# Perceiver block on one core: the next keys' steps one place forward, the next half's exponentials ahead of an eviction, the inverses' broadcast directly behind scores

## The chip, the core and the metric

The kernel runs on one core of a Trainium2 chip. The core has TensorE (PE, the matrix unit, whose weight loads are shown apart as PEld), VectorE (DVE), ScalarE (ACT), GpSimd (POOL) and SyncE (SP, which only starts DMAs here). The metric is the time of one execution on the device in microseconds, the median over runs. Each engine works through its own program in order and waits on semaphores for the others.

## The reference

One layer on `x` (32 images of 64 rows of 256) and a context (32 images of 1601 rows of 256). Most of the time goes into cross attention, which is followed by a small block with cosines and a running product, and by a mixture of experts.

```python
q = _split_heads(query @ Wq.T + bq)          # 16 heads of 16, query = layernorm(x)
k = _split_heads(key @ Wk.T + bk)            # key = value = ctx_1024
v = _split_heads(value @ Wv.T + bv)
score = jnp.einsum('bhqd,bhkd->bhqk', q, k) * SCALE
attn = jax.nn.softmax(score, axis=-1)
out = jnp.einsum('bhqk,bhkd->bhqd', attn, v)
...
x = x + _L0_xattn_ref(_layernorm(x, axis=-1), ctx_1024, ctx_1024, ...)
x = x + _L0_attn_ref(_layernorm(x, axis=-1), ...)
x = x + _L0_ffn_ref(_layernorm(x, axis=-1), ...)
```

The change touches only the cross attention.

## The kernel before

The attention runs over 32 images, and each image in two halves of eight heads: half `h` = 2n + m, 64 halves in all (`NH`). A half has four groups ("quads") i = 0 to 3 of four tiles of scores, 128 x 401 each. The functions named `period(h)`, one for each engine, say what an engine does between two halves; half `h` is finished in it and half `h + 1` is begun.

The way of a group through the engines:

- **Scores.** TensorE multiplies queries and keys (L965, 16 small matmuls on 32 x 32 tiles, into `a_pss`). VectorE takes them out of the four banks (L713, `take_scores`), with the maximum of each row on the way.
- **Maxima.** When all four groups of a half are taken, TensorE turns the row maxima (L974, `turn_max`), VectorE reduces them (L719, `reduce_max`), TensorE spreads the result (L980, `spread_max`), and ScalarE copies it as the bias of the exponentials (L504, `copy_bias`).
- **Exponentials.** ScalarE does four of 128 x 401 for each group (L498). VectorE turns each group (L728, `turn`, into `a_pT`). `a_pT` has 5 places, so the turn of group 1 of a half waits for the weighing of the half before.
- **Weighing.** TensorE multiplies the values by the turned exponentials (L994, `weigh`, 52 matmuls into `a_pso`). The sums of the exponentials are added up by TensorE (L1002, `total`), inverted by VectorE (L736, `invert`), laid out by GpSimd (L348, `spread_sums`), and broadcast by TensorE (L1010, `spread`). ScalarE evicts both (L513, `copy_out`), and GpSimd multiplies them (L357).
- In every fourth period, an odd one, TensorE also projects a finished tile (L1018, `project_out`), and VectorE adds the residual (L742 to L746, `residual`). Such an odd half is called one with a projection here.

In between, TensorE computes the keys and values of the next image in 15 steps, whose order is `STEP_ORDER`: a key step (K) is 6 matmuls of 416 columns, a value step (V) 12 of 256 columns (the last one 6), all on L925 to L927. In the order of the list the steps 0 to 3 are keys of the first half, 6, 8, 9 and 10 keys of the second half, and the others values. Each step fills one of two banks (`a_psk`, `a_psl`) and is copied by ScalarE (L526 keys, L533 and L535 values). A step waits until the step two before it is copied. `steps_in(h)` deals the steps to the four quarters of a period. The scores of group 0 of a half wait until the last key step of that half is copied: step 3 for the first half of an image, step 10 for the second.

```python
last_step = max(z for z, of in enumerate(order_of(n)) if of[0] == "k" and of[1] == m)
pe.wait_ge(kv_copied, STEPS * n + last_step + 1)
...
dve.wait_ge(exp_done, HALF * (at + 1))
if i == 1 and h > 0:
    dve.wait_ge(o_filled, h)
```

The order of all this is written out by hand in the four functions `period`; nothing plans it at run time.

Of the kernel before, what the change touches and what calls it, by code (L numbers as in the profile page):

```python
# [25 lines left out]
NH = NC * B  # L26
# [39 lines left out]
def quads(h):  # L66

    return ((1, 1), (0, 0), (0, 1), (1, 0)) if h % 2 else ((0, 0), (0, 1), (1, 0), (1, 1))
# [7 lines left out]
def steps_in(h):  # L76

    n = h // 2
    if h < 0:
        plan = [[(0, 4), (0, 5), (0, 6)], [(0, 7), (0, 8), (0, 9)], [(0, 10), (0, 11), (0, 12)], [(0, 13), (0, 14), (1, 0)]]  # L80
    elif h % 2 == 0:
        plan = [[(n + 1, 1)], [(n + 1, 2), (n + 1, 3)], [(n + 1, 4), (n + 1, 5)], [(n + 1, 6), (n + 1, 7), (n + 1, 8)]]
    else:
        plan = [[], [(n + 1, 9), (n + 1, 10), (n + 1, 11)], [(n + 1, 12), (n + 1, 13)], [(n + 1, 14), (n + 2, 0)]]
    return [[z for z in quarter if z[0] < B] for quarter in plan]


# [15 lines left out]
def attention_and_circuit(nc, ctxT, x, wq, bq, wk, bk, wv, bv, wp, rows, ident, marks, x1_scr, x1_mv, x1_by, x1_rs, x1_ex, w1, b1, w2, wr, rb, rows_scr,  # L103
                          wgu, wd, tri, counts):
    with ExitStack() as ctx:
# [383 lines left out]
        def _(act):  # L489
            def exponentials(h, i, some=range(HALF)):  # L490

                at = HALF * h + i
                e, r = quads(h)[i]
                act.wait_ge(bias_ready, h + 1)
                for j in some:
                    z = probs[:, at % RING, j, 0:KG]
                    at_bias = HALF * i + j
                    nc.scalar.activation(z, z, ACT.Exp, bias=bias[:, h % 2, at_bias:at_bias + 1], scale=-1.0,  # L498
                                         accum_out=esum[:, h % 2, j, 2 * e + r:2 * e + r + 1]).then_inc(exp_done, 1)

            def copy_bias(h):

                act.wait_ge(max_spread, h + 1)
                nc.scalar.copy(bias[:, h % 2, :], ps_m[:, P:P + HALF * HALF]).then_inc(bias_ready, 1)  # L504

            def copy_out(h):

                act.wait_ge(o_filled, h + 1)
                act.wait_ge(sums_filled, h + 1)
                if h > 1:  # L510

                    act.wait_ge(o_ready, h - 1)
                nc.scalar.copy(o_part[:, h % 2, :], ps_o[:, 0:2 * P]).then_inc(o_copied, 1)  # L513

            def copy_steps(steps):

                for n, s in steps:
                    at = STEPS * n + s
                    act.wait_ge(kv_filled, at + 1)
                    kind, *of = order_of(n)[s]  # L520
                    if kind == "k":
                        m, q = of
                        if n > 0:

                            act.wait_ge(s_filled, HALF * HALF * (NC * (n - 1) + m + 1))
                        nc.scalar.activation(keys[:, m, q * KG:(q + 1) * KG], step_bank(at)[:, 0:KG], ACT.Identity, bias=bk_sb[:, m:m + 1]).then_inc(kv_copied, 1)  # L526
                    else:
                        t = of[0]
                        if n > 1:

                            act.wait_ge(o_filled, NC * (n - 1))
                        if t < KT - 1:
                            nc.scalar.copy(v_of(n)[:, t:t + 2, :], step_bank(at)[:].rearrange("p (t d) -> p t d", t=2)).then_inc(kv_copied, 1)  # L533
                        else:
                            nc.scalar.activation(v_of(n)[:, t, :], step_bank(at)[:, 0:D], ACT.Identity, scale=mark[:, KEPT]).then_inc(kv_copied, 1)  # L535
# [16 lines left out]
            def angles(i):  # L552

                if i == 0 or i == UNITS - 1:
                    act.wait_ge(by_set, 6 if i == 0 else 12)
                act.wait_ge(x1_loaded[group_of[i]], 32 if i == UNITS - 1 else 16)
                if 2 * i + 1 >= KNOWN_IN:

                    act.wait_ge(kv_filled, STEPS * B)
                for t in range(2 * i, 2 * i + 2):  # L560
                    last = nc.scalar.activation(u[:, t, :], x1[:, t, :], ACT.Identity, bias=x1_by[:, 1, t:t + 1], scale=x1_by[:, 0, t:t + 1])
                last.then_inc(centred[0], 1)
# [22 lines left out]
            FORMER, LATTER = range(HALF // 2), range(HALF // 2, HALF)  # L585

            def period(h):
                steps = steps_in(h)
                if h >= 0:
                    exponentials(h, 1)  # L590
                copy_steps(steps[0])
                for i in ANGLES_IN.get((h, 1), ()):
                    angles(i)

                if h >= 0:
                    exponentials(h, 2)
                for i in ANGLES_IN.get((h, 2), ()):
                    angles(i)
                copy_steps(steps[1])

                if h >= 0:
                    exponentials(h, 3)
                for i in ANGLES_IN.get((h, 3), ()):
                    angles(i)
                copy_steps(steps[2])

                if h + 1 < NH:
                    copy_bias(h + 1)
                    exponentials(h + 1, 0, FORMER)
                copy_steps(steps[3][:1])  # L610
                if h > 0:
                    copy_out(h - 1)
                if h + 1 < NH:
                    exponentials(h + 1, 0, LATTER)
                copy_steps(steps[3][1:])

            for h in range(-1, NH):
                period(h)
# [14 lines left out]
            for stage, g in ACT_ORDER:  # L633
# [31 lines left out]
                elif stage == "copy_q":  # L665
                    n = GROUPS[g][1]
# [6 lines left out]
                elif stage == "relu":  # L673
                    i, j, g = g, g % FC, g // FC
                    n = GROUPS[g][1]
# [246 lines left out]
        def _(pe):  # L922
# [6 lines left out]
            def step(n, s):  # L929

                at = STEPS * n + s
                if at > 1:
                    pe.wait_ge(kv_copied, at - 1)
                if s == 0 and n > 0:
                    pe.wait_ge(ctx_split, NC * n)
                bank, slot = step_bank(at), n % 2
                kind, *of = order_of(n)[s]
                if kind == "k":
                    m, q = of
                    for k in range(NC):  # L940
                        mm = three(bank[:, 0:W], [w[:, 0, k, m * P:(m + 1) * P] for w in (w_hi, w_lo)],
                                   [c[:, slot, k].rearrange("p (t g a) -> p g t a", g=QK, a=32)[:, q] for c in (c_hi, c_lo)], k == 0, k == NC - 1)
                else:
                    for t in range(of[0], min(of[0] + TILES_A_STEP, KT)):
                        for k in range(NC):
                            mm = three(bank[:, (t % 2) * D:(t % 2 + 1) * D], [c[:, slot, k, P * t:P * (t + 1)] for c in (c_hi, c_lo)], [w[:, 1, k, :] for w in (w_hi, w_lo)], k == 0, k == NC - 1)
                mm.then_inc(kv_filled, 1)
# [117 lines left out]

            def period(h):
                steps = steps_in(h)

                if h + 1 < NH:
                    scores(h + 1, 2)  # L1070
                if h > 0:
                    weigh(h - 1)
                for z in steps[0]:
                    step(*z)

                if h > 0:
                    total(h - 1)
                if h + 1 < NH:
                    scores(h + 1, 3)
                if h % 4 == 1 and h > 4:  # L1080
                    project_out(h // 4 - 1)
                for z in steps[1]:
                    step(*z)

                if h + 2 < NH:
                    scores(h + 2, 0)
                if h + 1 < NH:
                    if h % 4 == 1 and h > 4:

                        pe.wait_ge(x1_ready, h // 4)  # L1090
                    turn_max(h + 1)
                for z in steps[2][:1]:
                    step(*z)
                if h + 1 < NH:
                    spread_max(h + 1)
                for z in steps[2][1:]:
                    step(*z)

                if h + 2 < NH:
                    scores(h + 2, 1)  # L1100
                for z in steps[3][:1]:
                    step(*z)
                if h > 0:
                    spread(h - 1)
                for z in steps[3][1:]:
                    step(*z)

            for h in range(-1, NH):
                period(h)
# [5 lines left out]
            for stage, g in PE_ORDER:  # L1115
# [8 lines left out]
                elif stage == "turn_q":  # L1124
                    t0, n = GROUPS[g]
# [9 lines left out]
                elif stage == "expand":  # L1135
                    i, j, g = g, g % FC, g // FC
                    t0, n = GROUPS[g]
# [8 lines left out]
                elif stage == "contract":  # L1146
# [5 lines left out]
                    for j in range(2):  # L1152
                        n = 2 * g + j - GROUPS[at][0]
# [678 lines left out]
```

## Time and profile before

| | us |
|---|---|
| median of 3 runs | 1748.42 (1747.88 to 1748.68) |
| profiled execution | 1745.66 |
| its span | 1743.9 |
| TensorE busy in the span | 1651.4 (95%) |
| VectorE busy | 1430.6 (82%) |
| ScalarE busy | 1218.2 (70%) |
| GpSimd busy | 948.6 (54%) |

The attention takes roughly the first 1300 us, some 36 to 37 us for each image. The rows shown below are from one image of the middle, about 699 to 747 us. In a timeline each row has the start, the time to the end of the last instruction of the row, the engine, the line, the operation, and in brackets the idle time ahead of it with what ended it. Matmuls overlap in the pipeline, so the cost of a step on TensorE is read from start to start, not from the length of a row.

### The profile page before, as it was taken

What the parts mean: (1) busy time and instruction counts of PE and PEld (TensorE: products, weight loads), DVE (VectorE), ACT (ScalarE), POOL (GpSimd) and SP (SyncE); (2) the same over time, 40 slices, a digit from 0 to 9 for tenths busy, and PEclk for the clock granted to TensorE, in tenths of its full rate; (3) what the DMA queues carried; (4) which work ended last, traced back from release to release, by engine and by line L of the source; (5) the groups of instructions that cost most, each with busy time, mean ns of one, the idle gap of its engine ahead of it and who ended that gap; (6) DMA issues with size and microseconds to landing.
All of it is one profiled execution on the core that took longest, in us unless ns stands there. A gap on an engine that the chain in (4) does not pass through costs nothing. (4 is left out here: it accounts for less than half of the span.)

```text
span 1743.9 us, 59225 instructions
## 1 busy us (share of the span) xinstructions
PE 1651.4 (95%) x24340; PEld 1352.1 (78%) x24340; DVE 1430.6 (82%) x3316; ACT 1218.2 (70%) x3297; POOL 948.6 (54%) x1427
## 2 busy tenths in 40 slices
PE   7999999999999999999999999996698899999998
PEld 4777777777777777777777777775476899999998
DVE  6698988989889898898888989889775776766657
ACT  3677877778777787777877788777555265656552
POOL 5355556555565555655556555553411448888850
PEclk9999999999999999999999999997797999999999
DMA  5011111211112111121111211111102356666632
GB/s 176 22 64 45 64 48 42 67 45 64 48 42 67 45 64 48 42 67 45 63 49 42 67 45 63 49 45 60 62 25 85 116 180 220 224 223 223 221 122 103
DMA packets 43439, 147.89 MB, mean 85 GB/s; under 512 B 5680, under 2 KB 25008, under 8 KB 39712
## 3 DMA queue, kind: packets, MB, share of 16 engines
q1 hardware_dynamic: 38416, 130.72, 21.9%
q0 software_dynamic: 4752, 13.38, 2.4%
q8 instruction: 192, 3.15, 0.7%
q14 instruction: 79, 0.65, 0.1%
HBM read 129.79 MB, written 14.16 MB: 83 GB/s over the span
## 5 line engine op out<-in xcount | busy, mean ns | idle before, releaser
L498 ACT ACTIVATE a_probs<-a_probs,a_bias 128x401 f32<-128x401 f32 x1024 | 632.0, 622 | 2.1
L728 DVE STREAM_TRANSPOSE a_pT<-a_probs 128x1664 f32<-128x1664 f32 x256 | 488.0, 1906 | 93.5 <-ACT a_probs L498 64.8
L713 DVE TENSOR_SCALAR_CACHE_REDUCE a_probs<-a_pss 128x401 f32<-128x401 f32 x1024 | 527.0, 570 | 25.6 <-PE a_pss L965 8.5
L965 PE MATMUL a_pss<-a_keys,a_qown 32*32 32x401 f32 x8192 | 253.2, 507 | 24.7 <-issue 23.4
L315 POOL TENSOR_TENSOR a_clo<-a_raw,a_chi 128x416 fp32r<-128x416 f32 x240 | 251.5, 1079 | 0.0
L994 PEld LDWEIGHTS a_pso<-a_pT,a_v 128*32 128x32 f32 x6656 | 182.2, 111 | 43.6 <-issue 40.5
L338 POOL TENSOR_SCALAR a_ex<-a_probs,a_marks 128x4 f32<-128x4 f32 x256 | 75.5, 295 | 253.2 <-ACT a_probs L498 252.9
L994 PE MATMUL a_pso<-a_pT,a_v 128*32 128x128 f32 x6656 | 199.7, 277 | 2.5 <-ACT a_op L513 2.1
L1661 PE MATMUL e_psg<-e_xh,e_guh 128*128 128x256 f32 x660 | 189.5, 287 | 5.5 <-DVE e_hl L1407 4.0
L498 ACT ACTIVATION_READ_ACCUMULATOR a_probs<-a_probs,a_bias 128x1 f32 x1024 | 194.4, 190 | 0.0
L1662 PE MATMUL e_psg<-e_xl,e_guh 128*128 128x256 f32 x660 | 186.7, 283 | 0.0
L1663 PE MATMUL e_psg<-e_xh,e_gul 128*128 128x256 f32 x660 | 186.5, 283 | 0.0
L357 POOL TENSOR_TENSOR a_op<-a_op 128x128 f32<-128x128 f32 x64 | 29.5, 461 | 236.8 <-ACT a_op L513 236.8
L1597 ACT ACTIVATE e_sg<-e_psg 128x256 f32<-128x256 f32 x180 | 68.9, 383 | 124.4 <-PE e_psg L1663 120.2
L1400 DVE TENSOR_TENSOR e_psg<-e_psg,e_sg 128x256 f32<-128x256 f32 x180 | 77.6, 432 | 80.7 <-ACT e_sg L1597 78.8
L526 ACT ACTIVATE a_keys<-a_psk,a_bk 128x401 f32<-128x401 f32 x127 | 75.1, 592 | 86.2 <-PE a_psk L927 85.7
L1661 PEld LDWEIGHTS e_psg<-e_xh,e_guh 128*128 128x128 f32 x660 | 125.6, 190 | 6.2 <-issue 6.2
L925 PE MATMUL a_psk<-a_whi,a_chi 128*128 128x256 f32 x420 | 127.3, 303 | 0.0
L1662 PEld LDWEIGHTS e_psg<-e_xl,e_guh 128*128 128x128 f32 x660 | 125.8, 191 | 0.0
L1663 PEld LDWEIGHTS e_psg<-e_xh,e_gul 128*128 128x128 f32 x660 | 125.7, 191 | 0.0
L925 PE MATMUL a_psl<-a_whi,a_chi 128*128 128x256 f32 x412 | 125.3, 304 | 0.0
L526 ACT ACTIVATE a_keys<-a_psl,a_bk 128x401 f32<-128x401 f32 x129 | 76.3, 592 | 64.7 <-PE a_psl L927 64.2
(253 smaller groups left out, 4249.9 us busy)
## 6 DMA issues: line engine op xcount, KB each, us to landing
a_raw<-in_ctxT SPq DMA_DIRECT2D x60, 832.0 KB, 4.4
f_gur<-in_wgu SPq DMA_DIRECT2D x24, 1408.0 KB, 6.5
f_dr<-in_wd SPq DMA_DIRECT2D x24, 768.0 KB, 4.7
e_big<-ys_scr SPq DMA_DIRECT2D x8, 512.0 KB, 7.3
a_probs<-in_ctxT SPq DMA_DIRECT2D x2, 1664.0 KB, 9.3
a_x<-in_x SPq DMA_DIRECT2D x16, 128.0 KB, 4.3
rows_scr<-f_a SPq DMA_DIRECT2D x8, 256.0 KB, 2.3
rows_scr<-f_a SPq DMA_DIRECT2D x4, 512.0 KB, 3.5
```

Source lines behind the costliest of these rows:

```text
L315: last = nc.gpsimd.tensor_tensor(out=c_lo[:, n % 2, k, cols], in0=src[:, cols], in1=c_hi[:, n % 2, k, cols].bitcast(F32), op=ALU.subtract)
L498: nc.scalar.activation(z, z, ACT.Exp, bias=bias[:, h % 2, at_bias:at_bias + 1], scale=-1.0, accum_out=esum[:, h % 2, j, 2 * e + r:2 * e + ...
L526: nc.scalar.activation(keys[:, m, q * KG:(q + 1) * KG], step_bank(at)[:, 0:KG], ACT.Identity, bias=bk_sb[:, m:m + 1]).then_inc(kv_copied, 1)
L713: nc.vector.tensor_scalar(probs[:, at % RING, j, 0:KG], ps_s[:, j, 0:KG], -SCALE, None, ALU.mult, ALU.min, accum_out=nmax[:, h % 2, at_max ...
L728: nc.vector.transpose(pT[:, turned_slot(h, i)].rearrange("p j k -> p (j k)"), probs[:, at % RING].rearrange("p j k -> p (j k)")).then_inc( ...
L925: nc.tensor.matmul(out, a[0], b[0], start=start, stop=False)
L965: mm = nc.tensor.matmul(ps_s[32 * g:32 * g + 32, j, 0:KG], q_own[32 * j:32 * j + 32, n % 2, m, e, 32 * r:32 * r + 32], keys[32 * j:32 * j ...
L994: mm = nc.tensor.matmul(ps_o[32 * j:32 * j + 32, 0:P], v_of(n)[:, t, 32 * p:32 * p + 32], pT[:, h % 2:h % 2 + HALF, j, 32 * t:32 * t + 32] ...
L1400: nc.vector.tensor_tensor(hidden(s, c), up, silu[0:P if c < EC - 1 else REST, c % 2, :], ALU.mult).then_inc(h_done, 1)
L1661: nc.tensor.matmul(out, a[0], b[0], start=start, stop=False)
L1662: nc.tensor.matmul(out, a[0], b[1], start=False, stop=False)
L1663: return nc.tensor.matmul(out, a[1], b[0], start=False, stop=stop)
```

## The change

`steps_in` deals each key and value step one place earlier: in an even period quarter 0 has step 2 instead of 1, quarter 1 has 3 and 4 instead of 2 and 3, quarter 2 has 5 and 6 instead of 4 and 5, quarter 3 has 7, 8 and 9 instead of 6, 7 and 8. In an odd period quarter 1 has 10 and 11 instead of 9, 10 and 11, quarter 2 is unchanged (12 and 13), and quarter 3 has 14 and then steps 0 and 1 of the image after. On TensorE the broadcast of the inverses (`spread`) stands directly behind the scores of quarter 3, ahead of all of that quarter's steps. On ScalarE the copy of the second step of quarter 2 moves behind the first two exponentials of the next half, and the last two exponentials move ahead of the first copy of quarter 3 and ahead of `copy_out`.

```diff
--- before.py
+++ after.py
@@ -77,11 +77,11 @@
 
     n = h // 2
     if h < 0:
-        plan = [[(0, 4), (0, 5), (0, 6)], [(0, 7), (0, 8), (0, 9)], [(0, 10), (0, 11), (0, 12)], [(0, 13), (0, 14), (1, 0)]]
+        plan = [[(0, 4), (0, 5), (0, 6)], [(0, 7), (0, 8), (0, 9)], [(0, 10), (0, 11), (0, 12)], [(0, 13), (0, 14), (1, 0), (1, 1)]]
     elif h % 2 == 0:
-        plan = [[(n + 1, 1)], [(n + 1, 2), (n + 1, 3)], [(n + 1, 4), (n + 1, 5)], [(n + 1, 6), (n + 1, 7), (n + 1, 8)]]
+        plan = [[(n + 1, 2)], [(n + 1, 3), (n + 1, 4)], [(n + 1, 5), (n + 1, 6)], [(n + 1, 7), (n + 1, 8), (n + 1, 9)]]
     else:
-        plan = [[], [(n + 1, 9), (n + 1, 10), (n + 1, 11)], [(n + 1, 12), (n + 1, 13)], [(n + 1, 14), (n + 2, 0)]]
+        plan = [[], [(n + 1, 10), (n + 1, 11)], [(n + 1, 12), (n + 1, 13)], [(n + 1, 14), (n + 2, 0), (n + 2, 1)]]
     return [[z for z in quarter if z[0] < B] for quarter in plan]
 
 
@@ -602,16 +602,16 @@
                     exponentials(h, 3)
                 for i in ANGLES_IN.get((h, 3), ()):
                     angles(i)
-                copy_steps(steps[2])
-
+                copy_steps(steps[2][:1])
                 if h + 1 < NH:
                     copy_bias(h + 1)
                     exponentials(h + 1, 0, FORMER)
+                copy_steps(steps[2][1:])
+                if h + 1 < NH:
+                    exponentials(h + 1, 0, LATTER)
                 copy_steps(steps[3][:1])
                 if h > 0:
                     copy_out(h - 1)
-                if h + 1 < NH:
-                    exponentials(h + 1, 0, LATTER)
                 copy_steps(steps[3][1:])
 
             for h in range(-1, NH):
@@ -1098,11 +1098,9 @@
 
                 if h + 2 < NH:
                     scores(h + 2, 1)
-                for z in steps[3][:1]:
-                    step(*z)
                 if h > 0:
                     spread(h - 1)
-                for z in steps[3][1:]:
+                for z in steps[3]:
                     step(*z)
 
             for h in range(-1, NH):
```

TensorE in an even half, at the scores of group 0 of the next image (`a_pss`, L965), which wait for the copy of step 3. Before:

```order
L925 MATMUL a_psl<-a_chi,a_whi 128x416
L926 MATMUL a_psl<-a_clo,a_whi 128x416
L927 MATMUL a_psl<-a_chi,a_wlo 128x416
L965 MATMUL a_pss<-a_keys,a_qown 32x401 x16
L974 MATMUL a_psm<-a_id,a_nmax 16x128
```

Now:

```order
L925 MATMUL a_psk<-a_whi,a_chi 128x256
L926 MATMUL a_psk<-a_wlo,a_chi 128x256
L927 MATMUL a_psk<-a_whi,a_clo 128x256
L965 MATMUL a_pss<-a_keys,a_qown 32x401 x16
L974 MATMUL a_psm<-a_id,a_nmax 16x128
```

The last key step no longer stands directly ahead of these scores; a value step (256 columns) stands between.

TensorE in an odd half, from the last scores of the next half (L965) into the steps that follow. Before:

```order
L965 MATMUL a_pss<-a_keys,a_qown 32x401 x16
L925 MATMUL a_psl<-a_chi,a_whi 128x416
L926 MATMUL a_psl<-a_clo,a_whi 128x416
L927 MATMUL a_psl<-a_chi,a_wlo 128x416
L925 MATMUL a_psl<-a_chi,a_whi 128x416
L926 MATMUL a_psl<-a_clo,a_whi 128x416
L927 MATMUL a_psl<-a_chi,a_wlo 128x416
L925 MATMUL a_psk<-a_chi,a_whi 128x416
```

Now:

```order
L965 MATMUL a_pss<-a_keys,a_qown 32x401 x16
L925 MATMUL a_psk<-a_chi,a_whi 128x416
L926 MATMUL a_psk<-a_clo,a_whi 128x416
L927 MATMUL a_psk<-a_chi,a_wlo 128x416
L925 MATMUL a_psk<-a_chi,a_whi 128x416
L926 MATMUL a_psk<-a_clo,a_whi 128x416
L927 MATMUL a_psk<-a_chi,a_wlo 128x416
L925 MATMUL a_psl<-a_whi,a_chi 128x256
```

One key step of the two between these scores and the value step has gone; the maxima's turn and spread further on (L974, L980) come one key step sooner.

TensorE in quarter 3 of an even half, from the scores to the broadcast (`a_pso<-a_sin`, L1010). Before:

```order
L965 MATMUL a_pss<-a_keys,a_qown 32x401 x16
L925 MATMUL a_psk<-a_chi,a_whi 128x416
L926 MATMUL a_psk<-a_clo,a_whi 128x416
L927 MATMUL a_psk<-a_chi,a_wlo 128x416
L925 MATMUL a_psk<-a_chi,a_whi 128x416
L926 MATMUL a_psk<-a_clo,a_whi 128x416
L927 MATMUL a_psk<-a_chi,a_wlo 128x416
L1010 MATMUL a_pso<-a_sin,a_marks 32x64 x8
L925 MATMUL a_psl<-a_whi,a_chi 128x256
```

Now:

```order
L965 MATMUL a_pss<-a_keys,a_qown 32x401 x16
L1010 MATMUL a_pso<-a_sin,a_marks 32x64 x8
L925 MATMUL a_psl<-a_whi,a_chi 128x256
L926 MATMUL a_psl<-a_wlo,a_chi 128x256
L927 MATMUL a_psl<-a_whi,a_clo 128x256
```

The broadcast follows the scores with no step between them.

ScalarE in an even half, from the last exponentials of half h, over the bias (L504), to the exponentials of half h + 1 (`a_probs`; the copies are `a_keys`, `a_v`, and `a_op` is the eviction). Before:

```order
L498 ACTIVATE a_probs,a_esum<-a_probs,a_bias 128x401 x4
L533 COPY a_v<-a_psk 128x512
L533 COPY a_v<-a_psl 128x512
L504 COPY a_bias<-a_psm 128x16
L498 ACTIVATE a_probs,a_esum<-a_probs,a_bias 128x401 x2
L526 ACTIVATE a_keys<-a_psk,a_bk 128x401
L513 COPY a_op<-a_pso 128x256
L498 ACTIVATE a_probs,a_esum<-a_probs,a_bias 128x401 x2
L533 COPY a_v<-a_psl 128x512
L526 ACTIVATE a_keys<-a_psk,a_bk 128x401
L498 ACTIVATE a_probs,a_esum<-a_probs,a_bias 128x401 x8
```

Now:

```order
L498 ACTIVATE a_probs,a_esum<-a_probs,a_bias 128x401 x4
L533 COPY a_v<-a_psl 128x512
L504 COPY a_bias<-a_psm 128x16
L498 ACTIVATE a_probs,a_esum<-a_probs,a_bias 128x401 x2
L526 ACTIVATE a_keys<-a_psk,a_bk 128x401
L498 ACTIVATE a_probs,a_esum<-a_probs,a_bias 128x401 x2
L533 COPY a_v<-a_psl 128x512
L513 COPY a_op<-a_pso 128x256
L526 ACTIVATE a_keys<-a_psk,a_bk 128x401
L526 ACTIVATE a_keys<-a_psl,a_bk 128x401
L498 ACTIVATE a_probs,a_esum<-a_probs,a_bias 128x401 x8
```

One copy moved from ahead of the bias to between the two pairs of exponentials, and the second pair now stands ahead of the eviction and of one copy.

## Rows read from the trace of the kernel before

**Rows 1.** The page: busy time by engine; TensorE's score matmuls.
```profile
PE 1651.4 (95%) x24340; PEld 1352.1 (78%) x24340; DVE 1430.6 (82%) x3316; ACT 1218.2 (70%) x3297; POOL 948.6 (54%) x1427
...
L965 PE MATMUL a_pss<-a_keys,a_qown 32*32 32x401 f32 x8192 | 253.2, 507 | 24.7 <-issue 23.4
```

**Rows 2.** Busy time by stretch: us, then PE, PEld, DVE, ACT, POOL, clock, DMA.
```profile
100.00:900.00 800.00, 783.91 (x14228) 603.25 (x14222) 714.98 (x1708) 632.28 (x1827) 453.25 (x803) 1.00 0.16 53
```

**Rows 3.** Waits of TensorE and VectorE, 100 to 900 us: total, times, longest.
```profile
PE a_pss L965 <- issue: 16.1, 22, 0.7
...
DVE a_pT L728 <- ACT a_probs L498: 44.1, 44, 1.6
...
DVE a_pT L728 <- PE a_pso L994: 19.9, 22, 0.9
```

**Rows 4.** Timeline of TensorE, an even half: start, us, engine, line, operation, idle before.
```profile
721.01 0.46 PE L925 MATMUL a_psl<-a_chi,a_whi 128*128 128x416 f32 x1
...
722.26 0.36 PE L925 MATMUL a_psk<-a_chi,a_whi 128*128 128x416 f32 x1
...
723.23 0.36 PE L927 MATMUL a_psk<-a_chi,a_wlo 128*128 128x416 f32 x1
...
724.32 0.97 PE L965 MATMUL a_pss<-a_keys,a_qown 32*32 32x401 f32 x32 [0.73 <-issue]
```

**Rows 5.** Timeline of ScalarE in the same half: key copies.
```profile
720.06 0.60 ACT L526 ACTIVATE a_keys<-a_psk,a_bk 128x401 f32<-128x401 f32 x1 [1.94 <-PE a_psk L927]
...
723.01 0.58 ACT L526 ACTIVATE a_keys<-a_psl,a_bk 128x401 f32<-128x401 f32 x1
...
723.63 0.59 ACT L526 ACTIVATE a_keys<-a_psk,a_bk 128x401 f32<-128x401 f32 x1
```

**Rows 6.** Timeline of TensorE, an odd half without a projection.
```profile
699.01 3.06 PE L994 MATMUL a_pso<-a_pT,a_v 128*32 128x128 f32 x104
...
704.20 0.35 PE L925 MATMUL a_psk<-a_chi,a_whi 128*128 128x416 f32 x1
...
705.35 0.28 PE L925 MATMUL a_psl<-a_whi,a_chi 128*128 128x256 f32 x1
...
706.87 0.96 PE L965 MATMUL a_pss<-a_keys,a_qown 32*32 32x401 f32 x32
...
709.40 0.25 PE L980 MATMUL a_psm<-a_id,a_low 16*32 16x16 f32 x8
```

**Rows 7.** Timeline of VectorE, the same odd half.
```profile
702.20 1.91 DVE L728 STREAM_TRANSPOSE a_pT<-a_probs 128x1664 f32<-128x1664 f32 x1 [0.92 <-PE a_pso L994]
...
708.13 0.28 DVE L719 TENSOR_REDUCE a_low<-a_psm 16x32 f32<-16x128 f32 x1
```

**Rows 8.** Timeline of VectorE, an odd half with a projection.
```profile
745.10 0.24 DVE L719 TENSOR_REDUCE a_low<-a_psm 16x32 f32<-16x128 f32 x1
```

**Rows 9.** Timeline of TensorE, the same half.
```profile
746.19 0.25 PE L980 MATMUL a_psm<-a_id,a_low 16*32 16x16 f32 x8
```

**Rows 10.** Timeline of TensorE around the spread inverses, an even half.
```profile
728.65 0.96 PE L965 MATMUL a_pss<-a_keys,a_qown 32*32 32x401 f32 x32
...
729.54 0.46 PE L925 MATMUL a_psl<-a_chi,a_whi 128*128 128x416 f32 x1
...
730.89 0.45 PE L1010 MATMUL a_pso<-a_sin,a_marks 32*32 32x64 f32 x16
...
731.27 0.39 PE L925 MATMUL a_psk<-a_whi,a_chi 128*128 128x256 f32 x1
...
734.06 0.96 PE L965 MATMUL a_pss<-a_keys,a_qown 32*32 32x401 f32 x32
```

**Rows 11.** Timeline of GpSimd, the same even half: the inverses laid out.
```profile
722.89 1.04 POOL L348 TENSOR_TENSOR a_sin<-a_inv,a_marks 32x512 f32<-32x512 f32 x1
```

**Rows 12.** Timeline of VectorE: one late start behind a transpose.
```profile
715.22 1.91 DVE L728 STREAM_TRANSPOSE a_pT<-a_probs 128x1664 f32<-128x1664 f32 x1 [0.83 <-ACT a_probs L498]
...
717.60 0.58 DVE L713 TENSOR_SCALAR_CACHE_REDUCE a_probs<-a_pss 128x401 f32<-128x401 f32 x1 [0.47 <-DVE a_pT L728]
```


## The prediction

> **What bounds the kernel now.** I read the page first, then the busy time of a long stretch of the attention, then the waits, then the timelines of single halves. The page has TensorE busy for 95% of the span, and most of the idle time ahead of its scores (L965) without a named releaser [rows 1]. In the stretch from 100 to 900 us it is busy for 783.9 of 800 us at a granted clock of 1.00 [rows 2]. The remaining 16.1 us are one wait alone: 22 times 0.73 us ahead of the scores on L965 [rows 3]. VectorE is busy for 715 of the 800 us, and its waits are for others: 44 times for the exponentials, 22 times for the weighing [rows 2, 3]. So the attention is a line of TensorE work with one hole for each image, and whatever shortens that line, or puts a new hole into it, moves the end. The stages behind the attention hold the same work as before and start when it ends; I carry each microsecond of the attention through to the end at full value.
>
> There is one such hole for each image, and an image takes 800 / 22 = 36.4 us [rows 3].
>
> **Term 1: the hole at the scores.** In the even half, TensorE starts step 2 at 721.01, step 3 at 722.26 and its last matmul at 723.23; the scores of group 0 start at 724.32, after 0.73 us idle [rows 4]. They wait for the copy of step 3, which ScalarE starts at 723.63 and ends 0.59 us later, at 724.22; TensorE goes on 0.10 us after that [rows 4, 5]. The change puts step 3 where step 2 was, and a value step where step 3 was. ScalarE's copies move with them: it copies step 2 at 720.06, where it waited 1.94 us for TensorE anyway, does four exponentials, and copies step 3 at 723.01, the start that the copy of step 2 has now [rows 5]. That ends at 723.60, and TensorE may go on at 723.70. TensorE itself is at the scores at 722.26 plus a value step that stands between a key step and scores, 706.87 - 705.35 = 1.52 us [rows 6], so at 723.78. The margin is 0.08 us: thin, but the hole closes. It is there in 31 of 32 images: 31 x 0.73 = **22.6 us less**. Bounds: all of it (22.6), or, if ScalarE is a few tenths late, 0.3 us of hole left in each image (13.3). I take 22.6, because ScalarE's start at 723.01 follows from the end of the exponentials and not from a wait. In the odd half the last key step (10) is already followed by a value step, before and now.
>
> **Term 2: the broadcast behind the scores.** A key step among other steps of its kind costs 705.35 - 704.20 = 1.15 us [rows 6]. The one that stands alone between scores and the broadcast costs 730.89 - 729.54 = 1.35 us [rows 10]. So it costs 0.20 us when a block of large matmuls is entered from small ones and left to small ones again. Now scores, broadcast and steps follow each other, and of the five blocks of steps in an odd half, and six in an even one, one goes in each: in quarter 3 two blocks become one. That is 0.20 us in each of 60 halves (the first has no broadcast, in the last ones there is nothing behind it): **12.0 us less**. What the scores cost ahead of large matmuls, 729.54 - 728.65 = 0.89 us [rows 10], is taken to stay ahead of the broadcast, which no row shows. Bounds: nothing (the broadcast pays behind scores what it saves elsewhere) and 12.0; I take 12.0, since both blocks around it are small matmuls on 32 x 32 tiles. The Trainium skill (TensorEngine Tiling, Tiling Modes, Key Properties) says that a change of the tiling mode drains TensorE. By that rule scores and broadcast, both 32*32, need no drain between them, and a step alone between them costs two; it would put all of the 0.20 us down to the two changes saved and speaks against the lower bound.
>
> **Term 3: the new hole.** In the odd half a key step leaves the stretch between the weighing and the spread of the maxima, so TensorE comes to L980 sooner by 1.15 us. VectorE cannot: its chain begins when the weighing ends. The weighing ends at 699.01 + 3.06 = 702.07; VectorE turns at 702.20, after 0.92 us idle for it, then inverts, takes four tiles, turns again and reduces the maxima at 708.13, with no idle time in between, until 708.41 [rows 6, 7]. All of this is fixed to the weighing. With the 0.10 us handover of term 1, TensorE may spread at 708.51. It does so at 709.40 now, and would come at 709.40 - 1.15 = 708.25 [rows 6]. It will wait 0.26 us. In an odd half with a projection VectorE also has the residual in the chain: the reduction ends at 745.10 + 0.24 = 745.34, TensorE may go on at 745.44 and comes at 746.19 - 1.15 = 745.04 [rows 8, 9]: 0.40 us (a part of it shows at the scores of group 0, whose banks are freed late). 16 x 0.26 + 15 x 0.40 = **10.2 us more**. In the even half nothing leaves that stretch except the old hole, and a value step takes a key step's place, so TensorE comes there later relative to VectorE than here. Bounds: 0 (the chain gains where I see no slack) to the whole cover, 1.15 us x 31 = 35.7 us; the rows put it at 10.2.
>
> **What costs nothing.** ScalarE does the same instructions in another order. The last two exponentials of group 0 move ahead of a copy and the eviction, so VectorE's 44 waits for them (1.0 us on average [rows 3]) shrink. That alone gives nothing: these waits are ahead of the turn of group 0, and the next thing in VectorE's line is the wait for the weighing, which TensorE sets. The value copy that moved behind the first pair of exponentials is needed by the second step after it, more than a key step away. The eviction comes 1.2 us later relative to the step's fill, and the next weighing, which needs it, is at least two steps further on (731.27 to 734.06 and one block of scores [rows 10]). If this cover went, each tenth of a microsecond would cost 6 us over 62 halves. The broadcast comes one step sooner, but the GpSimd instruction that feeds it ended at 722.89 + 1.04 = 723.93, and the scores ahead of the broadcast end after 729.5 [rows 10, 11]. No DMA is added or moved. Step 1 of the next image now also stands in the odd half; it reads the same context as step 0, which stands there before it, now as then.
>
> **The sum.** -22.6 - 12.0 + 10.2 = -24.4 us. The profiled execution took 1745.66 us for a span of 1743.9, so it would take 1721.3 for a span of 1719.5. The median of the runs lies 2.8 us above the profiled execution; from it, 1748.42 - 24.4 = **1724.0 us**.
>
> **The rivals.**
>
> *No new hole* (terms 1 and 2 in full, VectorE keeps up): 34.6 us less, 1713.8. For it: in the even half VectorE's line has slack, and its waits for the exponentials go. Against it: between 702.20 and 708.41 it has no idle time at all that could be given up [rows 7]. 12%.
>
> *Only half of it*: the hole closes to 0.3 us instead of nothing (13.3), the broadcast saves half (6.0), and the new hole is as in the sum (10.2): 9 us less, 1739.3; or term 2 is nothing and the rest is as in the sum: 12.4 less, 1736.0. For it: the margin of 0.08 us of term 1, and that no row shows a broadcast behind scores. 24%.
>
> *The hole only moves.* The new wait for the maxima takes back what the old one gave, because the chain behind the weighing is longer than I make it by 0.8 us in the odd halves: 0.33 + 0.8 = 1.13 us, against 0.73 + 0.39 for an image. 1748, no change. For it: 35.7 us of cover are removed. Against it: both odd halves read show 0.26 and 0.40. 7%.
>
> *Slower: VectorE's chain stretches.* One take started 0.47 us after the end of the transpose ahead of it (715.22 + 1.91 = 717.13, start 717.60) [rows 12], while it is 0.1 us or less elsewhere. If the new order of ScalarE and GpSimd made that the rule at the two places behind a transpose in the odd chain, the hole would be 0.33 + 0.94 = 1.27 us for an image, 0.15 more than the 1.12 that terms 1 and 2 give: 31 x 0.15 = 5 us slower, 1753. It decides from 0.79 us of stretch. Against it: the late start is one in 800 us in the trace. The Trainium skill (SBUF, its part on shared ports) says that a VectorE instruction with at most one SBUF input, outside its two-port modes, does not contend with GpSimd; the instructions in this chain are of that kind, so by it GpSimd's shifted work would not stretch them. 5%.
>
> **How the numbers follow.** Forecast as summed, 18 to 30 us less: 52%. With the rivals above that is 100%. The range has to leave out at most 2 in 10: from 1713, which takes in the full gain without a new hole, to 1740, which takes in the half gains; left out are the two last rivals and some of the tails. A measurement of this kernel tells 0.2%, about 3.5 us, from no change. Faster by more than that: forecast, no new hole and the half gains, 88%. Within it: 7%. Slower: 5%.
>
> **What would show it.** Step 1: the waits of TensorE from 100 to 900 us no longer have 22 x 0.7 us on L965 in the even half, and scores of group 0 follow the value step with no idle time. Step 2: the broadcast starts 0.9 us after the scores of quarter 3, and the key steps of that quarter run at 1.15 us start to start. Step 3: a new wait of TensorE at L980 (and some at L965) for VectorE in the odd half, 0.2 to 0.5 us, with VectorE's line from the turn to the reduction as long as now, 6.2 us. An image takes 800 / 22 - 0.79 = 35.6 us. I would be wrong if the hole at L980 were near 1 us, or if the scores of group 0 still waited for the copy of step 3.

## The result and the profile after

The changed kernel takes 1734.57 us (median of 4 runs, 1733.54 to 1736.70), beside 1748.55 us for the kernel before on the same chip: a ratio of 0.9923, 95% interval 0.9911 to 0.9935, so 11.4 to 15.6 us faster. The forecast was 24.4 us. The profiled execution took 1734.34 us, its span is 1732.5.

The page and the stretch from 100 to 900 us, against [rows 1, 2]:

```profile
PE 1661.8 (96%) x24340; PEld 1375.3 (79%) x24340; DVE 1425.3 (82%) x3316; ACT 1221.3 (70%) x3297; POOL 950.4 (55%) x1427
...
L965 PE MATMUL a_pss<-a_keys,a_qown 32*32 32x401 f32 x8192 | 273.9, 509 | 2.1 <-DVE a_probs L713 1.3
```

```profile
100.00:900.00 800.00, 800.00 (x14422) 627.01 (x14406) 719.01 (x1725) 640.51 (x1845) 460.56 (x813) 1.00 0.16 53
```

TensorE's waits are gone from this stretch, and it is called busy for all 800 us. That reads as if nothing could wait any more. Yet the page has 1661.8 us of matmuls where it had 1651.4, for the same 24340 instructions, and the scores on L965 alone went from 253.2 to 273.9 us. So a wait now lies inside a group of matmuls that is still called busy. The waits of VectorE and of the weight loads show it, against [rows 3]:

```profile
DVE a_pT L728 <- PE a_pso L994: 40.4, 45, 0.9
...
DVE a_probs L713 <- PE a_pss L965: 23.1, 23, 1.0
...
PEld a_pss L965 <- DVE a_probs L713: 10.3, 34, 0.3
```

VectorE does not wait for the exponentials any more, only for TensorE. And 34 weight loads of the scores waited for VectorE's takes. The kernel before has 22 such rows in the stretch, but of another kind: each stands ahead of a whole quad, for the 0.28 us that other quads show with no releaser named. From the kernel before:

```profile
714.72 0.23 PEld L965 LDWEIGHTS a_pss<-a_keys,a_qown 32*32 32x32 f32 x32 [0.28 <-DVE a_probs L713]
```

Of the 34 of the changed kernel 33 stand inside a quad, as shown further down: one in an odd half without a projection, two in one with it.

**The even half.** Timeline of TensorE, against [rows 4]: the key step 3, the value step, the scores of group 0.

```profile
716.28 0.46 PE L925 MATMUL a_psk<-a_chi,a_whi 128*128 128x416 f32 x1
...
717.54 0.28 PE L925 MATMUL a_psl<-a_whi,a_chi 128*128 128x256 f32 x1
...
719.07 0.96 PE L965 MATMUL a_pss<-a_keys,a_qown 32*32 32x401 f32 x32
```

The scores follow the value step with no idle time, 2.79 us after the key step's start where it was 3.31 with two key steps. ScalarE copies steps 2 and 3 as the forecast had it, 2.95 us apart [rows 5], and the copy of step 3 ends 0.20 us ahead of the scores, so with the handover of 0.10 us the margin is 0.10 us where the forecast had 0.08:

```profile
715.34 0.60 ACT L526 ACTIVATE a_keys<-a_psl,a_bk 128x401 f32<-128x401 f32 x1 [2.18 <-PE a_psl L927]
...
718.29 0.58 ACT L526 ACTIVATE a_keys<-a_psk,a_bk 128x401 f32<-128x401 f32 x1
```

**Quarter 3**, against [rows 10]: scores, broadcast, the first value step, and the next half's scores.

```profile
723.13 0.96 PE L965 MATMUL a_pss<-a_keys,a_qown 32*32 32x401 f32 x32
...
723.82 0.71 PE L1010 MATMUL a_pso<-a_sin,a_marks 32*32 32x64 f32 x16
...
724.46 0.38 PE L925 MATMUL a_psk<-a_whi,a_chi 128*128 128x256 f32 x1
...
728.39 0.96 PE L965 MATMUL a_pss<-a_keys,a_qown 32*32 32x401 f32 x32
```

**The odd half without a projection**, against [rows 6, 7]: on TensorE the weighing, the scores of group 0, the turn and the spread of the maxima; on VectorE the turn, the end of the last take and the reduction of the maxima.

```profile
693.88 3.06 PE L994 MATMUL a_pso<-a_pT,a_v 128*32 128x128 f32 x104
...
700.58 1.50 PE L965 MATMUL a_pss<-a_keys,a_qown 32*32 32x401 f32 x32
...
702.02 0.28 PE L974 MATMUL a_psm<-a_id,a_nmax 128*16 128x128 f32 x1
...
703.66 0.25 PE L980 MATMUL a_psm<-a_id,a_low 16*32 16x16 f32 x8
```

```profile
697.06 1.91 DVE L728 STREAM_TRANSPOSE a_pT<-a_probs 128x1664 f32<-128x1664 f32 x1 [0.94 <-PE a_pso L994]
...
701.07 0.08 DVE L713 DVE_READ_ACCUMULATOR a_probs<-a_pss 128x1 f32 x1
...
702.90 0.24 DVE L719 TENSOR_REDUCE a_low<-a_psm 16x32 f32<-16x128 f32 x1
```

The scores begin at 700.58, as early as one key step less allows, but the maxima are turned 1.44 us later and not 0.89: 0.55 us of hole, inside the scores. The spread of the maxima at 703.66 waits for nothing: VectorE's reduction ended at 703.14. With a projection it is 1.71 us, 0.82 us of hole, against [rows 8, 9] (TensorE, then VectorE from the residual to the end of the last take):

```profile
736.84 1.77 PE L965 MATMUL a_pss<-a_keys,a_qown 32*32 32x401 f32 x32
...
738.55 0.28 PE L974 MATMUL a_psm<-a_id,a_nmax 128*16 128x128 f32 x1
```

```profile
734.43 0.42 DVE L742 TENSOR_TENSOR a_x<-a_psm,a_x 128x256 f32<-128x256 f32 x1
...
735.46 0.24 DVE L736 RECIPROCAL a_inv<-a_pss 32x16 f32<-32x16 f32 x1
...
737.60 0.08 DVE L713 DVE_READ_ACCUMULATOR a_probs<-a_pss 128x1 f32 x1
```

What happens inside is seen on the weight loads. Of the changed kernel, the same odd half without a projection:

```profile
700.58 0.28 PEld L965 LDWEIGHTS a_pss<-a_keys,a_qown 32*32 32x32 f32 x24
...
701.21 0.15 PEld L965 LDWEIGHTS a_pss<-a_keys,a_qown 32*32 32x32 f32 x8 [0.34 <-DVE a_probs L713]
...
702.01 0.09 PEld L974 LDWEIGHTS a_psm<-a_id,a_nmax 128*16 128x16 f32 x1 [0.65 <-issue]
```

And of the kernel before, the corresponding half:

```profile
706.87 0.23 PEld L965 LDWEIGHTS a_pss<-a_keys,a_qown 32*32 32x32 f32 x32
...
707.76 0.09 PEld L974 LDWEIGHTS a_psm<-a_id,a_nmax 128*16 128x16 f32 x1 [0.65 <-issue]
```

Before, all 32 loads of the quad (the profile has two for each of the 16 matmuls) lie within 0.23 us: the four groups of four matmuls run side by side on their own rows of the array. Now 24 start at once and the last 8, for the fourth bank, 0.63 us later, 0.34 of it idle for VectorE's take. They start at 701.21, 0.06 us after VectorE has read the last tile (701.07 + 0.08 = 701.15), and the block behind them starts at 702.02, as a lone group takes nearly as long as four together: 0.87 us from the freed bank to the next block. With a projection the third group comes late too, but the last one decides: 737.60 + 0.08 + 0.87 = 738.55. In this half the turn of the maxima itself needs this last take, so these rows alone do not tell whether the scores or the turn was held; e7 does.

### The profile page after: what moved, and what is told of

Read it like the earlier page. It is cut to its first block and busy times, and to the rows that moved or that the text cites. A ratio compares the mean times of both kernels' runs of the same rounds, so it can differ in the third digit from the quotient of the medians.

```text
span 1732.5 us, 59225 instructions
## 1 busy us (share of the span) xinstructions
PE 1661.8 (96%) x24340; PEld 1375.3 (79%) x24340; DVE 1425.3 (82%) x3316; ACT 1221.3 (70%) x3297; POOL 950.4 (55%) x1427
## 5 line engine op out<-in xcount | busy, mean ns | idle before, releaser
L965 PE MATMUL a_pss<-a_keys,a_qown 32*32 32x401 f32 x8192 | 273.9, 509 | 2.1 <-DVE a_probs L713 1.3
```

The lines of the kernel that those rows point to most:

```text
L965: mm = nc.tensor.matmul(ps_s[32 * g:32 * g + 32, j, 0:KG], q_own[32 * j:32 * j + 32, n % 2, m, e, 32 * r:32 * r + 32], keys[32 * j:32 * j ...
```

## The experiments

An image's length, read from every second start of L974 (L984 in e5 and e10, whose kernels have ten lines more ahead of it) between 100 and 1150 us, repeats within 0.05 us in each kernel, but for a stray image here and there and the last one in some kernels, and parts the effects much better than the times do. In the table it stands for images without and with a projection.

| kernel | median us | ratio to before, 95% | image without, with |
|---|---|---|---|
| before | 1748.55 to 1749.66 | | 35.92, 36.78 |
| e1: steps only | 1743.89 | 0.9972 (0.9962 to 0.9982) | 35.66, 36.79 |
| e2: broadcast only | 1743.22 | 0.9967 (0.9955 to 0.9980) | 35.66, 36.52 |
| e3: exponentials only | 1748.22 | 0.9998 (0.9989 to 1.0007) | 35.92, 36.78 |
| the change | 1734.57 | 0.9923 (0.9911 to 0.9935) | 35.40, 36.52 |
| e9: the change, old exponentials | 1738.07 | 0.9943 (0.9929 to 0.9957) | 35.40, 36.60 |
| e5: the change, statistics later | 1726.18 | 0.9875 (0.9858 to 0.9892) | 35.40, 35.77 |
| e4: step 9 stays | 1712.37 | 0.9796 (0.9779 to 0.9813) | 34.85, 35.71 |
| e7: as e4, old exponentials | 1752.47 | 1.0017 (1.0008 to 1.0026) | 36.07, 36.93 |
| e8: as e4, step 2 joins 3 and 4 | 1707.04 | 0.9758 (0.9744 to 0.9771) | 34.53, 35.39 |
| e10: as e8, statistics later | 1711.89 | 0.9778 (0.9765 to 0.9792) | 34.53, 35.39 |

The times scatter more because of what follows. Up to 1110 us the granted clock of TensorE is 1.00 (2.4 GHz) in every stretch read here; behind that it falls at a place that differs from kernel to kernel. In e2 it is 0.91 from 1140 to 1160 us, where the kernels before and after the change have 1.00, and in e8 it is 0.91 from 1110 to 1130 us:

```profile
1140.00:1160.00 20.00, 18.86 (x306) 14.11 (x305) 15.51 (x37) 14.39 (x43) 7.75 (x17) 0.91 0.29 93
```

An image there took 39.67 us in e2 and 38.88 in e8. From the last turn of the maxima (1197.49 in the kernel before, so the attention ends nearer to 1230 than to 1300 us) to the end of the span it is 545.9 to 550.1 us in the eleven profiled executions. So a few microseconds between two times can come from there, and the images decide.

**e1, only the table `steps_in` as in the change; e2, only TensorE's broadcast; e3, only ScalarE's part of the diff.**

> Only the steps move one place forward; broadcast and ScalarE's order stay as before. Theory A (the four groups of scores of a quad run side by side, so the last bank has to be free when the first group starts; the hole in the odd half is 0.55 us, with a projection 0.82 us): the old hole of 31 x 0.73 = 22.6 us goes, the new one costs 16 x 0.55 + 15 x 0.82 = 21.1, so 1 to 2 us faster, within 0.2% of before. Theory B (the prediction's: the banks are needed one behind another, 10.2 us of new hole): 12 us faster, ratio 0.993. The scores of group 0 in an odd half take about 1.44 us to the turn of the maxima by A, 0.89 by B.

> Only the broadcast of the inverses moves behind the scores. From the trace of the changed kernel, 0.12 to 0.15 us saved in each of 60 halves: 8 us faster, ratio 0.9953. The prediction's 0.20 us would be 12 us, ratio 0.9931. A rival in which VectorE sets the pace of the attention would give less than 3 us, since TensorE would only wait longer elsewhere.

> Only ScalarE's order changes. Both theories: no change, within 1 us of before (ratio 0.999 to 1.001), with VectorE's waits for the exponentials of group 0 (44 us in 800) mostly gone and its waits for the weighing or the scores longer by the same amount. If ScalarE's order mattered by itself, it would be several us.

In e1 the scores of group 0 in the odd half take 1.44 and 1.71 us to the turn of the maxima, as in the changed kernel (TensorE, both odd halves; the turn follows the first of them at 707.50):

```profile
706.06 1.51 PE L965 MATMUL a_pss<-a_keys,a_qown 32*32 32x401 f32 x32
...
742.58 1.78 PE L965 MATMUL a_pss<-a_keys,a_qown 32*32 32x401 f32 x32
...
744.29 0.28 PE L974 MATMUL a_psm<-a_id,a_nmax 128*16 128x128 f32 x1
```

So the hole comes with the steps, not with the other two parts. e1 and e2 add up to the change in both kinds of image: -0.26 - 0.26 = -0.52, and 0.0 - 0.26 = -0.26. e3 moves nothing. The time of e1 is 5 us better than before and not 1 to 2 (by its images it is 16 x 0.26 = 4.2): I had put the closed hole at 0.73 us, and e4 shows it to be 0.81. e2 is 5.8 us better than before (3.5 to 7.9), a little less than the 8.1 us of its images, and what its profiled execution has in the image at 1140 us, 39.67 us against 37.84 in the kernel before, is of that size.

**e4, the key step 9 goes back to quarter 1 of the odd half,** all else as in the change.

```diff
-        plan = [[(n + 1, 2)], ..., [(n + 1, 7), (n + 1, 8), (n + 1, 9)]]
+        plan = [[(n + 1, 2)], ..., [(n + 1, 7), (n + 1, 8)]]
-        plan = [[], [(n + 1, 10), (n + 1, 11)], ...]
+        plan = [[], [(n + 1, 9), (n + 1, 10), (n + 1, 11)], ...]
```

> The changed kernel, but with step 9 in quarter 1 of the odd half, as before the change (even half: steps 2 to 8, odd half: 9 to 14, 0, 1). Theory A: the hole in the even half stays closed (22.6), the one in the odd half does not open, since the scores of group 0 start 1.15 us later there and all banks are free by then by 0.3 us or more; with 8 us for the broadcast, 31 us faster than before, ratio 0.9825, about 1718. Rival (VectorE's line of 33 us for an image is what TensorE runs into, and the hole opens at another of its waits): 10 to 20 us faster, with a wait of TensorE for L713 or L719 in some other place.

1712.37 us, 2.0% below before. TensorE, two turns of the maxima one image apart, and between them the scores of group 0 of the half with a projection, whose maxima are turned 0.89 us later (at 724.67):

```profile
706.90 0.28 PE L974 MATMUL a_psm<-a_id,a_nmax 128*16 128x128 f32 x1
...
723.78 0.96 PE L965 MATMUL a_pss<-a_keys,a_qown 32*32 32x401 f32 x32
...
742.61 0.28 PE L974 MATMUL a_psm<-a_id,a_nmax 128*16 128x128 f32 x1
```

The hole in the even half stays closed and none opens in the odd one. Of the 34 waits of the weight loads for VectorE's takes 2 are left, both ahead of whole quads:

```profile
PEld a_pss L965 <- DVE a_probs L713: 0.6, 2, 0.3
```

The time is 36.7 us below before (32.7 to 38.7), and the images give 33; 31 were expected. e4 against e2 gives what the closed hole is worth, 35.66 - 34.85 = 36.52 - 35.71 = 0.81 us (ScalarE's order differs too, but the rows of the kernel before give the same, 0.80, further down); e4 against the change gives what the new one costs, 0.55 and 0.81 us.

**e5, VectorE's statistics out of the line behind the weighing.**

```diff
                     if i == 1 and h % 4 == 1 and h > 4:
-                        residual(h // 4 - 1)
+                        add_up(h // 4 - 1)
                     if i == 2 and h + 1 < NH:
                         reduce_max(h + 1)
+                    if i == 2 and h % 4 == 1 and h > 4:
+                        statistics(h // 4 - 1)
```

> The changed kernel, with VectorE's two statistics instructions of the residual (L744, L746: 0.57 us of its line) moved from ahead of the inversion to behind the reduction of the maxima. Theory A (the hole in the odd half is the lateness of the last bank, plus the full length of one group of scores run alone): without a projection nothing changes, 35.40 us for an image and 0.55 us of hole; with a projection the last bank is free 0.57 us sooner and the hole shrinks from 0.82 to 0.25 us, 36.52 becomes 35.95 us. 15 x 0.57 = 8.6 us faster than the changed kernel, ratio to before about 0.987. Rival (the hole is a fixed cost of the new order of steps on TensorE, not VectorE's lateness): no change, ratio to before 0.992, 36.52 us for an image with a projection.

VectorE from the addition (now L747) to the end of the last take, and TensorE's scores (now L975) and turn (now L984), with a projection:

```profile
726.34 0.42 DVE L747 TENSOR_TENSOR a_x<-a_psm,a_x 128x256 f32<-128x256 f32 x1
...
726.68 0.23 DVE L736 RECIPROCAL a_inv<-a_pss 32x16 f32<-32x16 f32 x1
...
728.77 0.07 DVE L713 DVE_READ_ACCUMULATOR a_probs<-a_pss 128x1 f32 x1
```

```profile
728.75 1.02 PE L975 MATMUL a_pss<-a_keys,a_qown 32*32 32x401 f32 x32
...
729.70 0.28 PE L984 MATMUL a_psm<-a_id,a_nmax 128*16 128x128 f32 x1
```

From the start of the addition to the start of the inversion it is 0.34 us now and was 1.03: the two statistics also took the gaps around them along, so the image shrinks by more than the 0.57 us expected. The hole shrinks to 0.06 us (728.77 + 0.07 + 0.87 = 729.71), the image with a projection by 0.75 us, the one without by nothing. The lateness of the last bank, moved alone, moves the hole: the rival, a fixed cost of TensorE's order, is out.

**e7, e4 with ScalarE in its old order; e9, the change with it.**

> As e4_step9_stays, but ScalarE in its old order. Theory A: ScalarE's order is not on the path, so the time is that of e4 within 2 us (ratio to before 0.980), with VectorE's waits for the exponentials of group 0 back. Rival (at the shorter image VectorE has no room left, so its waits for late exponentials now reach TensorE): 5 to 30 us slower than e4, with TensorE waiting inside the scores of group 2 or ahead of the weighing.

> The changed kernel with ScalarE in its old order: steps and broadcast alone. The rule read from e7 (what follows a quad of scores starts 0.87 us after its last bank is freed, or 0.89 us after the quad's start, whichever is later) puts the scores of group 3 in the odd half one key step (1.15 us) later than in e7, where their hole was 1.2 us: 0.0 to 0.1 us of hole, so the time of the changed kernel within 2 us, ratio to before 0.992, 35.40 and 36.52 us for an image. Rival (late exponentials cost the same in any plan of steps): 1.2 us for an image as in e7, 37 us slower than the changed kernel, ratio 1.01.

My expectation of e7 was wrong, and its rival right in kind only: it had 5 to 30 us, and the wait inside the scores of group 2 or ahead of the weighing. e7 is 40 us slower than e4, which eats the whole gain and more, and the wait is inside the scores of group 3. Each image is 1.22 us longer. ScalarE (a value copy that waits for its step, the eviction, the last exponential of group 0), VectorE (the turn of that group, the end of the takes behind it) and TensorE (the scores of group 3, and the projection behind them), odd half:

```profile
735.27 0.58 ACT L533 COPY a_v<-a_psk 128x512 f32<-128x512 f32 x1 [0.93 <-PE a_psk L927]
...
735.75 0.38 ACT L513 COPY a_op<-a_pso 128x256 f32<-128x256 f32 x1
...
736.64 0.63 ACT L498 ACTIVATE a_probs<-a_probs,a_bias 128x401 f32<-128x401 f32 x1
```

```profile
737.39 1.91 DVE L728 STREAM_TRANSPOSE a_pT<-a_probs 128x1664 f32<-128x1664 f32 x1 [1.72 <-ACT a_probs L498]
...
741.40 0.08 DVE L713 DVE_READ_ACCUMULATOR a_probs<-a_pss 128x1 f32 x1
```

```profile
740.28 2.13 PE L965 MATMUL a_pss<-a_keys,a_qown 32*32 32x401 f32 x32
...
742.35 1.13 PE L1018 MATMUL a_psm<-a_wp,a_oT 128*128 128x256 f32 x4
```

The last exponential ends at 736.64 + 0.63 = 737.27 behind copy and eviction, VectorE turns the group at 737.39 after 1.72 us idle, the last take of group 2 ends at 741.48, and the scores of group 3 take 2.07 us instead of 0.92 (732.28 to 733.20 in the changed kernel): 741.48 + 0.87 = 742.35, the same rule at another place. Here the block behind the scores is the projection, which waits for none of VectorE's takes, so it is the scores that are held. Of the 1.22 us this is 1.15; the other 0.07 us are in the weighing ahead of it, 2.93 us from start to start and not 2.86. In e9 step 9 still stands ahead of these scores, 1.15 us of cover, and of the hole 0.08 us is left:

```profile
732.21 1.06 PE L965 MATMUL a_pss<-a_keys,a_qown 32*32 32x401 f32 x32
...
733.20 1.13 PE L1018 MATMUL a_psm<-a_wp,a_oT 128*128 128x256 f32 x4
```

e9 took 3.5 us more than the change, of which its images show 15 x 0.08 = 1.2 us; their intervals overlap. The rival, 1.2 us for every image, is out.

**e8, step 2 joins steps 3 and 4; e10, e8 with the later statistics.**

```diff
-        plan = [[(n + 1, 2)], [(n + 1, 3), (n + 1, 4)], ...]
+        plan = [[], [(n + 1, 2), (n + 1, 3), (n + 1, 4)], ...]
```

> As e4_step9_stays, but step 2 moves from quarter 0 of the even half to quarter 1, so that steps 2, 3 and 4 stand together and one block of large matmuls less is entered and left. If a block costs 0.13 us, as the broadcast alone showed (0.26 us for an image), the image takes 34.72 and 35.58 us instead of 34.85 and 35.71: 4 us faster than e4, ratio to before 0.977. Rival (VectorE or ScalarE is late somewhere when step 2 is later, since the weighing is then followed by scores at once, whose banks VectorE must have emptied): a hole of 0.5 us or more inside the scores of group 3, slower than e4.

> e8_step2_joins with the statistics of the residual behind the reduction of the maxima, as in e5. If no hole behind VectorE is left in the odd half of e8, nothing changes: 34.53 and 35.39 us for an image, ratio to before 0.976. If the image with a projection still held a part of VectorE's lateness, it would shrink by up to 0.57 us: 8 us faster, ratio 0.971.

TensorE in e8, even half: the sum, the scores of group 3 and the first of the three steps.

```profile
733.21 0.21 PE L1002 MATMUL a_pss<-a_sums,a_marks 128*32 128x16 f32 x2
...
733.35 0.99 PE L965 MATMUL a_pss<-a_keys,a_qown 32*32 32x401 f32 x32
...
734.26 0.46 PE L925 MATMUL a_psk<-a_chi,a_whi 128*128 128x416 f32 x1
```

The image is 0.32 us shorter than in e4, not 0.13: a lone block of a key step costs about 0.2 us extra, as in term 2 of the prediction, and the weighing is now followed by another block of small matmuls, which makes it 0.12 us shorter (from 2.99 to 2.87 us, start to start). e8 is the fastest, 2.4% below before; its median is 5.3 us below that of e4, and its images give 9.9. e10 has the same images, so no lateness of VectorE is left in e8. Its median is 5 us higher, with intervals that overlap, while the two profiled executions are alike (1711.47 in e8, 1711.89 in e10); why the medians differ stays open.

## Why the prediction was right in its sign and half wrong in its size

- **Term 1, 22.6 us less.** It held, at 0.81 us for an image (25.1 us). The 0.08 us more is the way idle time is counted: from the modelled end of the last matmul. The scores could have started at 723.23 + 0.29 = 723.52, as blocks behind a key step do, and started at 724.32 [rows 4].
- **Term 2, 12.0 us less.** Measured 0.26 us for an image, 8.1 us by the images. The key step's 0.20 us was right. The scores' 0.89 us, which the term let stand, was not: the broadcast starts 0.69 us behind them, but the step behind it starts 0.64 us later and not 0.38, together 1.33 us where 0.89 + 0.38 = 1.27 was assumed. The Trainium skill (TensorEngine Tiling, Tiling Modes, Key Properties) says that changing the tiling mode, not just the tile, drains TensorE. Read as in the prediction, it would have let all 0.20 us stand; the trace gives 0.13 for a half.
- **Term 3, 10.2 us more.** This is the step that failed. The chain was right: VectorE's line from the weighing to the reduction has no slack, and the lost key step exposes it. Place and size were wrong. I looked for the hole at the spread of the maxima, named the late banks of the scores only in passing, and never asked when the fourth bank has to be free. The four groups start together, so the bank is needed at once, and a late group takes nearly the full time of the quad from the moment its bank is free. By that rule the hole is 701.15 + 0.87 - (700.58 + 0.89) = 0.55 us, and 0.82 with a projection: 16 x 0.55 + 15 x 0.82 = 21.1 us, twice the term. The Trainium skill says on the same page that different tiles execute weight loads and matmuls in parallel; the weight loads agree (32 within 0.23 us before, 24 and then 8 now). The trace of the kernel before already had the lateness: the last take ended at 706.29, 0.58 us ahead of the scores at 706.87 [rows 6], so with a key step less, 1.15 us, it comes 0.57 us late.

```profile
706.21 0.08 DVE L713 DVE_READ_ACCUMULATOR a_probs<-a_pss 128x1 f32 x1
```

- **The sum.** -25.1 - 8.1 + 21.1 = -12.1 us; the runs show -14.0 (11.4 to 15.6). The prediction's rival "only half of it" has about this number (9 and 12.4 us less), by causes that did not occur. So 1734.57 us lies in the range to 1740 only because the range had room for these, and that is luck.
- **The signs.** The even half and the key steps of quarter 3 came as said. The broadcast started 0.69 us after the scores and not 0.9, and the new wait at L980 did not come: it was 0.55 and 0.82 us at the scores of group 0 instead.
- **"Costs nothing".** ScalarE's order is worth nothing in the kernel before (e3) and at most 0.08 us for an image with a projection in the changed one (e9). It was right for this change, and it would have been 40 us wrong to carry it on: with step 9 back in place it is what keeps VectorE ahead (e7).

## What to carry to other kernels

When small matmuls run side by side on their own rows, ask of each of their buffers whether it is free when the first of them starts, not when its turn in the program comes: here the late group then ran alone and took nearly as long as all four together, so 0.57 us of lateness cost 0.55 us. Moving work forward past a wait also takes it away from another place; before it goes, look at what it covered there. An edit that does nothing by itself can be what makes the next one pay, so test it once more together with that one.

## What was not expected of the hardware

A quad of 16 score matmuls takes 0.89 us from its start to the next block when all its banks are free, and its last quarter alone 0.81 us from its first weight load (701.21 to 702.02). In such a stall the profile calls TensorE busy: 800 of 800 us in the changed kernel, with 21 us of holes over the attention. They show here as busy time that grew for the same number of instructions, and as idle time of the weight loads.
